# Attention: three query tiles in the last step of a group and five spread over the next steps, with scores that wait for one tile

## The reference

```
    xn = layer_norm(x, ln_g, ln_b)
    cn = layer_norm(context, cln_g, cln_b)
    q = (xn @ Wq).reshape(b, n, HEADS, DIM_HEAD).transpose(0, 2, 1, 3) * scale
    k, v = jnp.split(cn @ Wkv, 2, axis=-1)              # one key and value head of 64 for all 16 heads
    sim = jnp.einsum('bhid,bjd->bhij', q, k) + mask[:, None, :, :]
    attn = jax.nn.softmax(sim, axis=-1)
    out = jnp.einsum('bhij,bjd->bhid', attn, v)
    out = out.transpose(0, 2, 1, 3).reshape(b, n, INNER) @ Wout
    val, gate = jnp.split(xn @ W1, 2, axis=-1)
    return out + jax.nn.silu(gate) * val @ W2
```

## Time and profile before

| | |
|---|---|
| median of 3 runs | 1914.57 us (1913.03 to 1915.65) |
| profiled execution, its time | 1913.43 us |
| its span in the profile | 1911.6 us |
| TensorE busy | 1800.1 us, 94% |
| VectorE, ScalarE, GpSimd busy | 1285.3, 925.4, 418.2 us |
| query tiles (L1483, `x_wq`) | 256 matmul records, 99.5 us |
| scores (L1438) | 896 records, 202.5 us; 23.7 us of idle time before them |

### The profile page before, as it was taken

How to read it: one execution, slowest core, us unless ns; L and a number is a source line. 1 busy time by engine, 2 the same in 40 slices (tenths; PEclk the granted TensorE clock), 3 DMA queues, 4 the chain that set the end, 5 groups by cost and what they waited for, 6 DMA issues and landing times.

```text
span 1911.6 us, 28245 instructions
## 1 busy us (share of the span) xinstructions
PE 1800.1 (94%) x9512; PEld 1056.6 (55%) x9512; DVE 1285.3 (67%) x3970; ACT 925.4 (48%) x2262; POOL 418.2 (22%) x569
## 2 busy tenths in 40 slices
PE   4389999999999998999999999999999999999997
PEld 2266676676677544454554554544545554555466
DVE  6578888888885578367567647647746656764743
ACT  3334634544541456445545545545645644554542
POOL 4748678677773001000000000000000000000000
PEclk8689999999999999999999999999999999999999
DMA  4000000000002324223222222223222222223200
GB/s 128 1 1 11 11 11 11 20 11 11 11 29 77 116 77 150 53 63 76 68 63 68 62 66 71 63 61 77 63 58 75 69 63 67 65 63 69 53 13 20
DMA packets 73007, 102.46 MB, mean 54 GB/s; under 512 B 10304, under 2 KB 67584, under 8 KB 71968
## 3 DMA queue, kind: packets, MB, share of 16 engines
q1 hardware_dynamic: 72400, 100.20, 19.6%
q10 hardware_dynamic: 464, 0.46, 0.1%
HBM read 93.25 MB, written 7.39 MB: 53 GB/s over the span
## 4 chain that ended last, share of the span: by engine, by line
PE 90%; DVE 6%; ACT 1%; issue 1%; DMA 1%; SPq 0%; DVEq 0%; ACTq 0%
PE ps L1483 20%; PE ps L1438 9%; PE ps L1445 9%; PE ps L1476 9%; PE ps L1461 8%; PE ps L293 7%; PE ps L430 6%; PE ps L412 4%; PE ps L376 4%; PE ps L392 3%; PE ps L1543 2%; PE ps L1583 1%; PE ps L1537 1%; PE ps L362 1%; PE ps L1549 1%
## 5 line engine op out<-in xcount | busy, mean ns | idle before, releaser
L1822 DVE CUSTOM_DVE_ANT_0 x_pr<-ps,x_mk 128x375 f32<-128x375 f32 x448 | 227.7, 546 | 310.3 <-issue 198.5
L1694 ACT ACTIVATE x_pT<-ps 125x384 f32<-125x384 f32 x448 | 195.4, 489 | 265.1 <-PE ps L1445 264.2
L1700 ACT ACTIVATE x_pr<-x_pr,x_mx 128x375 f32<-128x375 f32 x448 | 268.1, 607 | 36.8 <-DVE x_mx L1822 36.5
L1445 PEld LDWEIGHTS ps<-ident,x_pr 128*125 128x125 f32 x1344 | 163.8, 187 | 129.5 <-issue 89.9
L1438 PE MATMUL ps<-x_kT,x_qT 64*128 64x375 f32 x896 | 202.5, 527 | 23.7 <-DVE x_mx L1822 17.7
L1445 PE MATMUL ps<-ident,x_pr 128*125 128x128 f32 x1344 | 206.1, 289 | 0.1
L1483 PE MATMUL ps<-x_xn,x_w 128*128 128x448 f32 x512 | 203.8, 541 | 0.0
L1831 DVE TENSOR_SCALAR x_pr<-x_pr,x_rc 128x375 f32<-128x375 f32 x448 | 169.9, 422 | 8.0
L1461 PE MATMUL ps<-x_pT,x_va 125*64 125x512 f32 (+1 forms) x768 | 160.0, 552 | 0.6 <-ACT x_pT L1694 0.6
L293 PE MATMUL ps<-m_xa,w_in 128*128 128x448 f32 x352 | 145.7, 561 | 5.7 <-ACT m_xa L525 5.7
L1438 PEld LDWEIGHTS ps<-x_kT,x_qT 64*128 64x128 f32 x896 | 68.2, 184 | 144.0 <-issue 114.7
(11 more groups left out here) (198 smaller groups left out, 2910.0 us busy)
## 6 DMA issues: line engine op xcount, KB each, us to landing
x_mk<-in_mask SPq DMA_DIRECT2D x224, 187.5 KB, 2.4
x_cx<-in_context SPq DMA_DIRECT2D x32, 375.0 KB
x_cT<-in_context_turned SPq DMA_DIRECT2D x32, 375.0 KB, 3.2
x_rb<-context_roots SPq DMA_DIRECT2D x32, 187.5 KB, 5.2
x_mixed<-m_x SPq DMA_DIRECT2D x8, 448.0 KB, 3.4
X<-x_mixed SPq DMA_DIRECT2D x8, 448.0 KB, 4.0
m_X<-in_x SPq DMA_DIRECT2D x7, 448.0 KB, 4.0
out<-f_so SPq DMA_DIRECT2D x7, 448.0 KB, 3.4
```

The lines of the kernel that those rows point to most:

```text
L1445: last = pe.transpose(bank(2 + e)[0:JP, t * ROWS:(t + 1) * ROWS], pr[:, 2 * (p % SLOT) + e, t * JP:(t + 1) * JP], ident[:, :])
L1694: act.activation(pT[:, 2 * NV * (batch(p) % 2) + 2 * (p % NP % NV) + e, :, :].rearrange("p t s -> p (t s)"), bank(2 + e)[0:JP, 0:JT * ROWS ...
L1700: act.activation(pr[:, k, :], pr[:, k, :], ACT.Exp, scale=-1.0, bias=mx[:, k:k + 1], accum_out=sums[:, k:k + 1]).then_inc(h_e.sem, 1)
L1822: dve.tensor_tensor_reduce(pr[:, k + e, :], bank(e)[:, 0:J], mk[:, p % SLOT, :], -1.0, 3.0e38, ALU.add, ALU.min, mx[:, k + e:k + e + 1]).t ...
```

## The change

`schedule` puts only the first three query tiles (`QUERIES` = 3) into step 27; tiles 3 to 7 are put into slot X of steps 0 to 4 of the group that uses them. In the last group's list `AHEAD`, which it leaves out, only tiles 0 to 2 are left, and tiles 3 to 7 join `BEHIND`, so that group 0, whose tiles all come from `START`, skips them. The scores of step 0 wait for tiles 0 and 1, those of steps 1 to 6 for tile p + 1 each. Everything computed is the same.

```
     for b in range(GB):
         for r, kind in ((NP - 2, "kv"), (NP - 1, "vback")):
             at[(b - 1) % GB * NP + r, "X"].insert(0, (kind, b))
-    at[STEPS - 1, "Y"] += [("query", n) for n in range(KA)]
+    at[STEPS - 1, "Y"] += [("query", n) for n in range(QUERIES)]
+    for n in range(QUERIES, KA):
+        at[n - QUERIES, "X"].append(("query", n))
     return at
 
 
 W1_AT = 10
+QUERIES = 3
...
-AHEAD = [piece for piece in START if piece[0] != "mlp"]
+STARTED = [piece for piece in START if piece[0] != "mlp"]
+AHEAD = [piece for piece in STARTED if piece[0] != "query" or piece[1] < QUERIES]
...
-          + [("up", n) for n in range(KH)] + [("down", 0), ("down", 1)])
+          + [("up", n) for n in range(KH)] + [("down", 0), ("down", 1)] + [("query", n) for n in range(QUERIES, KA)])
...
-        self.start, _ = self.places(AHEAD)
-        self.first, n0 = self.places([("start",) + x for x in AHEAD] + [x for x in body if x not in BEHIND])
+        self.start, _ = self.places(STARTED)
+        self.first, n0 = self.places([("start",) + x for x in STARTED] + [x for x in body if x not in BEHIND])
...
-            if p == 0:
-                for n in (KA - 2, KA - 1):
-                    emptied(pe, i - 1, ("query", n))
+            for n in range(2) if p == 0 else (p + 1,) if p < NP else ():
+                emptied(pe, i - 1 if n < QUERIES or i == 0 else i, ("query", n))
```

## The result

The changed kernel took 1903.35 us (median of 5 runs, 1902.62 to 1904.92) beside 1914.57 us before (5 runs, 1913.03 to 1917.17): a ratio of 0.9941, interval 0.9926 to 0.9955, so 0.59% or 11.2 us faster. The forecast was 1905.3 us. The direction and the mechanism were right, and the gain was larger by 2 us; the time lies at the lower end of the range, by the ratio just outside it. The two profiled executions have spans of 1911.6 and 1900.8 us, 10.8 us apart.

What follows compares the result with a forecast made beforehand. TensorE was taken to bound the attention groups. Seven boundaries (8.05 us), 0.26 us more at groups 0 and 1, and the start (1.0 us) gave 9.3 us off, so 1905.3 us against the 1914.57 median; range 1903.3 to 1909.0.

Steps and rivals of the forecast that it cites:

- the range: Whole-kernel time of 1903.3 to 1909.0 us, given chance 0.85; it left out dearer waits, lost cover and the clock.
- What bounds the kernel: In the eight attention groups, TensorE, busy 152.59 of 155.00 us; only its last 2 to 3 us per group can move.
- The boundary, 16.64 to 15.49 us: Between groups, TensorE's query tiles to step 1's output projection, plus three later tiles: 1.15 us less at each of seven boundaries.
- Checks (a) to (d): At group boundaries: four checks that tile evictions, VectorE and later scores would not be late, with 0.85 to 5.4 us spare.
- VectorE's cover: Before scores of step 0: of VectorE's 11.73 us idle time, the change takes 8.27 us and 3.46 us stay.
- (a): Scores of step 0: tile 1's eviction ends before the three tiles do, with 0.85 us to spare.
- The start, 1.0 us: In front of group 0: first scores need only tiles 0 and 1, so start at 648.48 instead of 649.49 us.
- The price of the waits: On TensorE, six more waits in a group, 48 in all, were taken to cost 0.
- The rival with 0.1 us everywhere: On TensorE's queue: all 48 added waits cost 0.1 us each, giving 1910.1 us; chance 0.07.
- The clock in steps 0 to 4: TensorE's granted clock in the steps given one tile each was expected to stay at 1.00.
- the sum: Whole kernel: seven boundaries 8.05 us, 0.26 us more at groups 0 and 1, start 1.0 us; together 9.3 us.
- the prediction's only rival on the clock: At boundaries: without the dense burst, TensorE gets 1.2 instead of 2.4 GHz, 78 us in seven, 1983 us; chance 0.02.

## Why the prediction came out as it did

- *What bounds the kernel*: right. All that the change itself gained lies in TensorE's waits ahead of scores, and nothing else became late.
- *The boundary, 16.64 to 15.49 us*: right, 10.98 us for the first part and 1.14 us less in a group. The waits alone gave 0.74 us of it for the eighth eviction, less the 0.11 us that scores 1 lose; filling the loop gave the rest.
- *Checks (a) to (d)*: right. VectorE's cover was put at 3.46 us and was 3.50. Tile 3 was put at 4.0 us after scores 0 and was 3.94. There is no wait for `x_qT`. Two tiles show how close (a) is: there it fails.
- *The start, 1.0 us*: 0.90 in its row. The prediction had 1.60 us from the last tile's start to scores that don't wait, as between other tiles, and here it is 1.70. Of the 0.90 us 0.12 are lost again in the next loop, 0.08 of them to the added wait. This was the one term for which I took the price of a wait from steps that don't wait.
- *The price of the waits*: 0 was right for 47 of 48. The rival with 0.1 us everywhere had the size nearly right and the places wrong.
- *The clock in steps 0 to 4*: right, 1.00. The advice of the Trainium skill (Perfetto Trace Analysis, section Matmul Optimizations) to run matmuls back to back in batches would have spoken against the change. The rows show no loss from the splitting: with the batch spread, TensorE's rows still stand back to back, and it is busy 13.03 of 13.03 us in the steps with one tile each.
- *The step that failed*: the sum. It was made against the profiled execution's own time as if all outside the boundaries and the start stood still, so that the end had a term of nothing without a reason. That execution had a fall of the granted clock at the end (0.50 for 3 us), worth 1.69 us, and I never asked whether a kernel that arrives there 9 us earlier would meet it again; the prediction's only rival on the clock was about the boundaries, and only about a loss. In three of three traces of the kernel before the fall is there, and in none of three of the changed kernel. The terms that the sum did have came to 9.1 us where it had 9.3. With the 1.7 us that is 10.8 us, the difference of the two profiled executions; the medians differ by 11.2.
- *The range*: its lower end lay 2 us under the forecast and held neither that fall nor the beginning of the attention: the last query tile ahead of it started between 646.02 and 649.33 us in executions of kernels whose mixer is the same. With these two in it, it would have begun at 1902 or less, by my estimate from these numbers.

What stays open is why the clock falls in one kernel and not in another. Take the end of the 2.05 us, counted from the first scores. The fall came where this was 1214.48 to 1214.96 us (three traces of before) and 1199.29 us (tile 0 in step 26). It did not come where it was 1206.30 to 1206.77 us (three traces of after, four tiles, the start put back), 1210.07 us (waits alone), 1216.40 us (one tile twice) and 1217.53 us (two tiles). It repeated in the two kernels that have several traces; what it hangs on was not found.

## What to carry to other kernels

When a consumer waits for the last of a burst of producers, narrow the wait to the piece that it needs, and leave in the burst just as many pieces that the needed one's eviction is done when the burst ends; the others can fill loops elsewhere that are waits now. An added wait cost nothing here where TensorE was still at work, and 0.08 us where it stood still. Measure a gain of this size from landmark to landmark inside the part that changed, and ask of each clock fall in the trace before whether the shifted kernel will still meet it.

## What the runs showed of the hardware

- The same idle time of 2.05 us ahead of the same work was followed by a fall of the granted clock in four of the twelve traces that have it and not in eight (4.88 or 3.19 us for sixteen records of 224 columns). With 1.5 us of work added some 630 us earlier, the one trace taken had no fall.
- A wait added to an instruction that stands still at another wait delays its start by 0.08 us (from 0.61 to 0.69 us between VectorE's operation and the scores), seen at the boundary and at the start; scores in the same traces without an added wait kept 0.60 or 0.61 us.
- The part ahead of the attention, the same in all kernels, ended anywhere in 3.3 us (start of the last query tile 646.02 to 649.33 us) from one execution to the next, nearly a third of the effect under study. All of it arises in the first 155 us, at a mean granted clock of 0.77 to 0.80; the 494.4 us behind, at 1.00, agree within 0.04 us.
